# A chain of graph layers on one core: polynomial and convolutions worked pair by pair, with half of each row cast by VectorE and half by ScalarE

## The reference, cut to what matters

```python
# layer 0: attention-like messages, summed by receiver
# layer 1, three passes:
lx = x - spmm(x, src, dst, dinv[src] * w * dinv[dst])
x = hh + proximal_l21(x - lx - hh, gamma * 0.1)
# layer 2, a polynomial of degree 5:
result = c[0] * x; tx = x
for k in range(1, 6):
    tx = segment_sum(norm[:, None] * tx[col], row)   # row = src, col = dst
    result = result + c[k] * tx
# layer 3, twice (relu after the first):
h = x @ W
agg = segment_sum(h[src] * (dinv[src] * dinv[dst])[:, None], dst)
x = agg + h / deg + b
```

## Time and profile before

| | us |
|---|---|
| median of three runs | 8615.32 |
| the profiled execution | 8620.85 |
| its span, first to last instruction | 8619.2 |
| TensorE busy (matmul) | 6966.2 (81%) |
| VectorE busy | 5906.5 (69%) |
| ScalarE busy | 4550.4 (53%) |
| GpSimd busy | 2850.0 (33%) |
| clock granted to TensorE, mean | 0.944 |

### The profile page before, as it was taken

One profiled execution on the slowest core, in us unless ns is written; L12 is line 12 of the kernel. 1 busy time (PEld: TensorE's weight loads), 2 busy tenths in 40 slices (PEclk: granted clock), 3 DMA queues, 4 the chain that ended last, 5 costly groups with the idle time before them and its releaser, 6 DMA issues. The chain is left out here.

```text
span 8619.2 us, 280713 instructions
## 1 busy us (share of the span) xinstructions
PE 6966.2 (81%) x98149; PEld 5903.7 (68%) x98174; DVE 5906.5 (69%) x15840; ACT 4550.4 (53%) x14713; POOL 2850.0 (33%) x2937
## 2 busy tenths in 40 slices
PE   0299999999999899999956886877867787875876
PEld 0155555555555699999956776877867777875866
DVE  1277676766777699898966886886885555555555
ACT  0222222222222499999956997987974444433443
POOL 0078888888888655454530000000000000000000
PEclk9999999999999999999978998999988898987978
DMA  9222222222222377777747887887965454542534
GB/s 385 89 57 61 59 59 60 58 61 58 60 59 59 110 233 232 225 231 223 232 141 232 285 281 244 286 280 253 290 208 167 164 171 157 179 156 90 182 126 134
DMA packets 781195, 1429.84 MB, mean 166 GB/s; under 512 B 294298, under 2 KB 361580, under 8 KB 776696
## 3 DMA queue, kind: packets, MB, share of 16 engines
q1 hardware_dynamic: 571720, 967.63, 36.0%
q10 hardware_dynamic: 116928, 381.29, 12.8%
q0 software_dynamic: 92048, 74.42, 4.4%
HBM read 987.87 MB, written 433.30 MB: 165 GB/s over the span
## 5 line engine op out<-in xcount | busy, mean ns | idle before, releaser
L243 POOL DMA_INDIRECT sorted_rows<-sort_rows,sort_row_at x1600 | 1989.5, 1243 | 518.4 <-issue 507.1
L1458 ACT ACTIVATE smooth_msg<-smooth_ps_l,smooth_w_rows 128x64 f32<-128x64 f32 x7500 | 1592.1, 404 | 229.0 <-PE smooth_ps_l L1522 215.4
L272 ACT ACTIVATE sort_count<-sort_ps_c 50x50 bf16<-50x50 f32 x1600 | 331.2, 207 | 1995.4 <-PE sort_ps_c L304 1559.0
L1216 PE MATMUL poly_ps<-parts,poly_cast 125*128 125x192 bf16 x12500 | 1088.5, 252 | 201.9 <-DVEq L1295 106.3
L1216 PEld LDWEIGHTS poly_ps<-parts,poly_cast 125*128 125x128 bf16 x12500 | 1071.6, 100 | 218.6 <-issue 135.4
L1182 ACT ACTIVATE poly_cast<-poly_mat 128x1280 bf16<-128x1280 uint8 x500 | 609.3, 1262 | 767.9 <-PE poly_ps L1216 520.0
L1522 PE MATMUL smooth_ps_l<-parts,smooth_src 125*128 125x64 bf16 x22500 | 798.5, 194 | 260.5 <-DMA smooth_src<-src_rows 163.7
L1522 PEld LDWEIGHTS smooth_ps_l<-parts,smooth_src 125*128 125x128 bf16 x22500 | 717.7, 99 | 298.0 <-ACT smooth_msg L1458 110.9
L314 PE MATMUL sort_ps_m<-sort_w,sort_hidden 128*125 128x64 f32 x3200 | 879.3, 430 | 0.0
L1536 PE MATMUL smooth_ps_s<-smooth_msg,smooth_hot 128*128 128x64 bf16 x7500 | 760.3, 194 | 143.7 <-DVE smooth_last_part L1670 119.0
L300 PEld LDWEIGHTS sort_ps_r<-sort_count,sort_hot_dt 50*125 50x125 bf16 x1600 | 283.0, 177 | 847.2 <-issue 643.8
...
## 6 DMA issues: line engine op xcount, KB each, us to landing
...
graph_edges<-sorted_rows SPq DMA_DIRECT2D x125, 700.0 KB
...
hot_rows<-graph_hot SPq DMA_DIRECT2D x125, 640.0 KB, 3.4
src_rows<-graph_hot_t SPq DMA_DIRECT2D x125, 640.0 KB, 3.7
```

Of the source, the lines that this page charges most:

```text
L243: pool.indirect_dma_start(out=sorted_rows, out_offset=bass.IndirectOffsetOnAxis(row_at[u][:, j:j + 1], 0), in_=rows[u][:, j, :], in_offset ...
L1216: last = nc.tensor.matmul(ps[u][:, 0:3 * D], cast[u][h][0:NL, s, :], parts[:, b].rearrange("p i d -> p (i d)"), start=b == 0, stop=b == NB ...
L1458: last = act.activation(at[:, s, :], ps_l[g % 2][h][:, i * D:(i + 1) * D], ACT.Copy, scale=w_rows[:, u, c * CHUNK + s:c * CHUNK + s + 1])
```

## The change

What it does:

- **Spilled edges, in all ten passes**: a class `Spilled` works them in rounds of two tiles (250 edges); `n_pairs` is counted beside `n_spilled` in the sort, which also stores one more block of zero rows behind them. GpSimd does the edge load, the cast of the indices, the two gathers, the two additions and the load of `y_sb`; the zeroing of `y_rows` for the next pass follows that load, and the first one stands before the first pass. ScalarE issues the write of the node table.
- **Polynomial and convolutions**: the passes are unrolled, with the structure of smoothing. VectorE casts blocks 0 to 24 of a row in one operation, ScalarE blocks 25 to 49 in one. SyncE issues the loads, each half after its engine's cast of two rows before. The small steps of a finished pair of rows stand behind each cast: four at a time for pairs 6 to 19, all of a pair's for each row of pairs 20 to 24. Spilled edges are worked after pair 2. Rows 0 and 1 of a pass run up to block 47 while the last pairs' steps are still running.
- **A node's own value** is added by TensorE, with an identity, in smoothing and the convolutions.
- **Smoothing**: ScalarE scales the first eight blocks of a chunk, VectorE the last two in one operation, ahead of the second subtraction of the chunk before. The loads are of blocks 0 to 19 and 20 to 49 of a row, with two row buffers; `ADD` is 3; steps stand in pairs 4 to 21 one at a time, in 22 to 24 two at a time.
- `hh` becomes a view of `node_sums`, and `sums` and `rest` share memory with a second `parts`.

The core of the diff:

```diff
@@ sort_edges
-                link(dve.tensor_scalar(pad_f[:], so_far[:], 1.0 / TE, -0.496, ALU.mult, ALU.add), at + 2)
+                dve.tensor_scalar(pad_f[:, 0:1], so_far[:], 1.0 / TE, -0.496, ALU.mult, ALU.add)
+                link(dve.tensor_scalar(pad_f[:, 1:2], so_far[:], 0.5 / TE, -0.498, ALU.mult, ALU.add), at + 2)
...
@@ class Spilled (new)
+    def write_table(self, eng, xs):
+        eng.dma_start(self.rows.rearrange("(p b) d -> p (b d)", b=NB), xs[:].rearrange("p b d -> p (b d)"))\
+           .then_inc(self.table, 16)
+    def on_pool(self, pool, k, n, y_sb):
+        pool.wait_ge(self.table, 16 * k + 16)
+        pool.wait_ge(self.zeroed, 16 * k + 16)
+        with pool.Fori(0, n) as t:
+            m = k * n + t
+            pool.dma_start(self.edges[:], self.sorted_rows[bass.ds(N_SLOTS + t * (2 * TE), 2 * TE), :]
+                           .rearrange("(i p) c -> p i c", i=2)).then_inc(self.got, 16)
+            pool.wait_ge(self.got, m * 16 + 16)
...
+            for i in range(2):
+                pool.indirect_dma_start(out=self.of_node[:, i, :], out_offset=None, in_=self.rows,
+                                        in_offset=bass.IndirectOffsetOnAxis(self.from_at[:, i:i + 1], 0))\
+                    .then_inc(self.fetched, 16)
+            pool.wait_ge(self.ready, m + 1)
+            for i in range(2):
+                pool.indirect_dma_start(out=self.y_rows, ..., compute_op=ALU.add).then_inc(self.added, 16)
+                pool.wait_ge(self.added, m * 32 + (16 * i + 16))
+        pool.dma_start(y_sb[:].rearrange("p b d -> p (b d)"), ...).then_inc(self.y_in, 16)
...
@@ spread
-    N2 = 24
-    DVE_S = 15
+    SPILL_AT, LATE, TWICE = 2, 6, 20
+    EARLY = NB - 2
...
+            def _(sp):
+                def pair(k, p):
+                    for u in two:
+                        for h in two:
+                            if not at_start(k, p):
+                                sp.wait_ge((cast_v, cast_a)[h], number(k, p, u) - 1)
+                                sp.sem_inc(taken, 1)
+                            load(..., u, h)
...
+            def _(act):
+                def pair(k, p):
+                    for u in two:
+                        if not at_start(k, p):
+                            act.wait_ge(row_done, number(k, p, u) - 1)
+                        act.wait_ge(loaded[u][1], k * 16 * PAIRS + 16 * p + 16)
+                        act.activation(cast[u][1][:], mat[u][1][:], ACT.Copy).then_inc(cast_a, 1)
+                for k in range(n_passes):
+                    pair(k, 0)
+                    act.wait_ge(posted, PAIRS * (k + 1))
+                    spilled.write_table(act, xs)
+                    with act.Fori(1, PAIRS) as p:
+                        pair(k, p)
...
+            def _(pe):
+                def first_pair(k):
+                    for u in two:
+                        if k > 0:
+                            pe.wait_ge(row_kept, number(k, 0, u) - 1)
+                        blocks(k, 0, u, 0, EARLY)
+                    pe.wait_ge(posted, PAIRS * k + PAIRS)
+                    for u in two:
+                        last = blocks(k, 0, u, EARLY, NB)
+                        if own_edges:
+                            last = own(k, 0, u)
+                        last.then_inc(row_done, 1)
...
+            def _(dve):
+                def cast_half(k, p, u):
+                    dve.wait_ge(loaded[u][0], k * 16 * PAIRS + 16 * p + 16)
+                    dve.tensor_copy(cast[u][0][:], mat[u][0][:]).then_inc(cast_v, 1)
+                def pair(k, p, by_row, at_once, ahead):
+                    for u in two:
+                        dve.wait_ge(row_done, number(k, p, u) + 1)
+                        dve.tensor_reduce(one_row(sums, p, u), ps[u][0:NL, 0:3 * D]...).then_inc(row_kept, 1)
+                        if not isinstance(p, int) or p < PAIRS - 1:
+                            cast_half(k, p + 1, u)
+                        elif k < n_passes - 1:
+                            cast_half(k + 1, 0, u)
+                        by_row[u].go(at_once)
...
@@ smooth
-    ADD = 2
-    SPILL_AT, LATE, TWICE = 1, 3, 23
+    ADD = 3
+    SPILL_AT, LATE, TWICE = 1, 4, 22
...
-                    for h in two:
-                        act.wait_ge(looked, 2 * number + (h + 1))
-                        for i in range(HALF):
...
+                    act.wait_ge(looked_a, number + 1)
+                    for i in range(BY_ACT):
+                        last = act.activation(at[:, i, :], ps_a[g % 2][:, i * D:(i + 1) * D], ACT.Copy,
+                                              scale=w_rows[u][:, c * CHUNK + i:c * CHUNK + i + 1])
+                    last.then_inc(scaled_a, 1)
...
+                def scale(k, p, u, c):
+                    number = N_CHUNKS * row_of(k, p, u) + c
+                    dve.wait_ge(looked_v, number + 1)
+                    if c == 0:
+                        dve.wait_ge(w_kept, row_of(k, p, u) + 1)
+                    if not (isinstance(number, int) and number < RING):
+                        dve.wait_ge(chunk_done, number - (RING - 1))
+                    dve.tensor_tensor(msg[c][:, BY_ACT:CHUNK, :], ps_v[...]..., w_rows[u][...]..., ALU.mult)\
+                       .then_inc(scaled_v, 1)
...
-                            dve.wait_ge(scaled, 2 * number + 2)
+                            dve.wait_ge(scaled_a, number + 1)
+                            dve.wait_ge(scaled_v, number + 1)
                             dve.tensor_tensor(rest[c][:], msg[c][:], high(msg[c]), ALU.subtract).then_inc(firsts, 1)
+                            if c + 1 < N_CHUNKS or u == 0:
+                                scale(k, p, u + (c + 1) // N_CHUNKS, (c + 1) % N_CHUNKS)
...
@@ polynomial
-            link(dve.tensor_tensor(sums[:], sums[:], y_sb[:], ALU.add))
-            link(dve.tensor_tensor(sums[:], sums[:], wide(dis), ALU.mult))
...
+            link(dve.tensor_tensor(z[:], sums[:, b, :], y_sb[:, b, :], ALU.add))
+            for u in range(2):
+                last = dve.scalar_tensor_tensor(row, z[:, u, :], one_row(by_coeff[:, k, :], p, u), row, ALU.mult, ALU.add)
+            link(last)
+            link(dve.tensor_tensor(xs[:, b, :], z[:], twice[:, b].unsqueeze(2).to_broadcast([NL, 2, D]), ALU.mult))
...
```

776 lines of the change are left out of this document (395 added, 381 removed).

## The result

| | before | after |
|---|---|---|
| median, us | 8612.14 (4 runs) | 8154.54 (4 runs, 8147.68 to 8169.89) |
| ratio | | 0.9472, 95% interval 0.9455 to 0.9488 |
| up to smoothing (profiled execution) | 4500.8 | 4489.3 |
| smoothing, to the next layer norm | 1915.5 | 1768.1 (-147.4; forecast -30) |
| polynomial | 1454.9 | 1228.8 (-226.1; -192) |

Faster by 5.3%. A stage in the table runs from the start of one layer norm to the start of the next. By pass, smoothing took 30.6, 39.4 and 77.4 us less.

What follows compares the result with a forecast made beforehand. It took ScalarE as smoothing's first limit, VectorE close behind, and TensorE, with 70 us a pass not full-rate multiplication, in the polynomial. 8620.85 - 192 (polynomial) - 50 (convolutions) - 30 (smoothing) = 8349, less 5.5: 8343 us; range 8225 to 8450.

Steps and rivals of the forecast that it cites:

- I take 24.1: 12.05 a row: Smoothing's middle rows: VectorE's time for a pair of rows after the change, in us, making VectorE the bound.
- 7 the steps, 0.34 for one between two big ones: Smoothing: of VectorE's 21.8 us a pair before, 7 are small steps, each 0.34 between two big operations.
- 0 to 0.15 per chunk for the second wait: Smoothing: us added to VectorE's time by a second wait ahead of each subtraction.
- 10 x 0.21 to 0.36: Smoothing: us added to VectorE's pair of rows by ten scalings of the last two blocks of a chunk.
- -20 to -25, +18 and +11: Smoothing, us a pass: first eight rows gain 20 to 25, 36 middle rows lose 18, last six lose 11.
- Rival 1: Smoothing: engine waits make the 11.56 us rows, deeper buffers bring 11.2; another -110 us, total 8235; chance 0.14.
- The 4 us for low clock: Polynomial: us charged to each pass for TensorE's lower clock after the short pauses, within the 237.8.
- 38.8 x 5, less 2 at the ends: Polynomial: 38.8 us saved in each of five passes, less 2, giving the stage's -192.
- the 5 for low clock: Convolutions: 5 us added to each for low clock and last steps, within the -25 each.
- rival 2: y_sb lands late, so VectorE waits at pair 6 in polynomial, convolutions and smoothing: +60 us, total 8400; chance 0.18.
- Rival 3: Polynomial and convolutions: VectorE bounds the rows, 4.5 us instead of 4.13; +130 with doubled pairs, total 8475; chance 0.10.
- Rival 4: Smoothing: VectorE, TensorE and ScalarE wait in a ring each chunk, rows of 14.1 us, total 8630; chance 0.04.

Runs made afterwards that it cites:

- run 2: The changed kernel with ScalarE scaling 7 of a chunk's 10 blocks in smoothing and VectorE 3, in place of 8 and 2: 8191.55 us, ratio 0.9512.
- Run 1: The changed kernel with two of smoothing's semaphores counted by 2 and by 3, so waits ask for different values but come no earlier or later: 8256.29 us, ratio 0.9587.
- run 3: The changed kernel with smoothing's row buffers reloaded only after 5 or 7 chunks of the next rows, in place of 2 and 5: 8250.3 us, ratio 0.9573.

## Why the prediction missed, point by point

**The step that failed** is "I take 24.1: 12.05 a row", VectorE's pair of rows in smoothing. It is 21.88. Who bounds the row was right (run 2). Of its terms:
- "7 the steps, 0.34 for one between two big ones": steps priced as the trace of before had them. A step costs 0.09 less ahead of `last_part` in the changed code (0.34, now 0.25) and 0.10 less ahead of `rest` (0.55, from 4906.91 to 4907.46, now 0.45): 14 of them are 1.3 a pair. Between step and big operation the kernel before lists an operation of 46 ns (L1666) or 40 ns (L1669), the changed one none; it has operations of 40 ns at the waits of the scaling instead (L1763, L1767), the first at 4912.6, where `rest` starts. The kernel before:

```profile
4906.91 0.41 DVE L1630 TENSOR_SCALAR xs<-smooth_z,dinv 125x64 f32 x2
L1666 DVEq FUSED_REGOPS  x156: 46/46/81, 4700.0 to 5099.2; - x156
L1669 DVEq ALU_OP  x173: 40/40/40, 4701.1 to 5098.0; - x173
```

- "0 to 0.15 per chunk for the second wait": nothing; behind the step at 4912.18 `rest` starts 0.04 us after its end, and nothing is listed at L1780. Run 1 takes both back at once, and the pair is 23.9, my 24.1; smoothing is then 1865.6 where I forecast 1885.5.
- "10 x 0.21 to 0.36" for the scaling: 0.20, just under the lower bound, which was the reading of the nearest row. I had taken some 0.05 more each: 0.5 a pair.

The step's 1.3, the second wait's 0.7 (run 1's 2.0 less 1.3) and the scaling's 0.5 are 2.5, for the 2.2 that the pair was off; the 0.3 over are not taken apart.

Over the 36 rows of a pass this is 40 us, and passes 0 and 1 came out 30.6 and 39.4 shorter where I had 0. (My own terms for them, -20 to -25, +18 and +11, make +4 to +9 and not 0.) The doubled rows went the same way, 13.2 us for the 14.2 forecast. The two bounds I gave for smoothing (-130 and +90) didn't hold its -147 either: the price of the steps stood in them as fixed. For pass 2, I had 11.0 a row and it was 9.84. Run 1, with the old price of a step, has 10.44 (20.87 / 2), so that price explains 0.6 of the 1.2. The other 0.6 is that I took off only 2.1 a pair for five steps fewer, where run 1 shows 3.0. Rival 1 named the gain and gave the wrong cause, though the deeper buffers are what lets pass 2 have it (run 3).

**Smoothing's first rows**: forecast -20 to -25 us a pass; rows 0 to 7 went from 127.3 to 109.7 in pass 1 and from 127.3 to 111.0 in pass 2, and less in pass 0 (124.4 to 115.3). So the gain was 9 to 18, short of the forecast. The rows themselves are at 10.5 to 17.8, not 10; the transfers of `y_sb`, the zeroing and the table still stand beside them.

**Polynomial, four passes**: 233.5 us each where I had 237.8. By intervals over 4.125, means of the four: boundary 5.1 (4.5), doubled rows 2.9 (4), spilled edges 6.6 (5.5), transfers 5.5 table + 4.2 `y_sb` + 3.0 zeroing = 12.7 (13.5); with 206.3 these make 233.5. The 4 us for low clock have no place beside them. The rows of before show the first half of why. These are PE, PEld, DVE, ACT, POOL, the granted clock, DMA by stretch, around the pause of the earlier trace rows:

```profile
7012.00:7039.00 27.00, 0.90 (x11) 0.67 (x9) 25.18 (x10) 2.43 (x2) 0.00 (x0) 0.55 0.09 30
7039.00:7046.00 7.00, 6.51 (x63) 6.41 (x64) 2.97 (x4) 0.71 (x1) 0.00 (x0) 0.77 0.53 167
7046.00:7053.00 7.00, 7.00 (x88) 7.00 (x86) 2.58 (x4) 2.08 (x3) 0.00 (x0) 1.00 0.67 234
```

Of the 155 us of clock that the stage lost before (0.89 of 1386 us), TensorE was multiplying in 58; in the rest it stood still, as in the four pauses between passes, with 0.54 to 0.62 granted. After a pause of 27 us it lost 0.23 x 7 = 1.6 us. Around the changed boundary:

```profile
6560.00:6565.00 5.00, 2.16 (x18) 2.09 (x19) 4.44 (x17) 0.00 (x0) 0.00 (x0) 0.85 0.50 172
6565.00:6570.00 5.00, 4.62 (x45) 4.30 (x42) 0.69 (x3) 0.13 (x1) 0.00 (x0) 0.81 0.27 102
```

These lose 0.15 x 5 and 0.19 x 5, 1.7 us. The second half of why is in the changed kernel, one pass long:

```profile
6570.00:6800.00 230.00, 213.71 (x2484) 210.62 (x2485) 157.12 (x307) 142.94 (x50) 15.05 (x8) 0.97 0.63 199
```

It does lose 0.03 x 230 = 7 us a pass to the clock, nearly all of it while TensorE multiplies. By the clock's own record these are some 1.7 us each in the intervals at the boundary, at the late table rows, at the spilled edges and at `y_sb` (passes 1 to 3). In the kernel before, the intervals of the earlier trace rows, from which I priced all but the boundary, held such a loss already; I charged it again, beside them.

**The last pass of the polynomial**: "38.8 x 5, less 2 at the ends". With its end it took 217.5 us, 18 less than 237.8 - 2. It has no boundary, no doubled rows at 4.45, no zeroing beside it; its end is 4.0 us. These terms belonged to four passes, not five. **Convolutions**: -82.4 for -50, so 16 more each. Their rows are 4.21, 0.09 over, as forecast (4.1 a pass), and the 5 for low clock is lost (0.98 of 228 us above) but inside the other intervals, as in the polynomial. The transfers were the larger miss: by the intervals, the four first rows of each convolution stood 13.6 to 14.0 us over full rate and now stand 2.3 over, and the two at `y_sb` 8.5 to 9.5 and now 4.2 to 4.6. These are 16 us each where I had 7.

**`y_sb`** (rival 2): no instruction of VectorE waits for `y_sb` in the after trace, and it landed in 12.3 us. GpSimd's part of an addition is longer beside casts, though. One pass, GpSimd in order of time:

```profile
6599.62 2.04 POOL L1189 DMA_INDIRECT y_rows<-poly_total,poly_to  x1 [7.10 <-DVE poly_total L1240]
6604.55 3.29 POOL L1189 DMA_INDIRECT y_rows<-poly_total,poly_to  x1 [2.89 <-DMA y_rows<-poly_total,poly_to]
```

The first addition of each polynomial pass, with no cast beside it, keeps GpSimd busy for 2.04 us, the second, which has one, for 2.86 to 3.56; before it was 2.0 and 3.0. Why it is longer no run here shows, and the 0.8 to 1.5 us a transfer delayed nothing that anything waited for. **Rival 3** (rows of 4.5 in the polynomial) holds in the doubled rows alone. **Rival 4** (ring of waits): rows at 10.9. **The scaling**: an operation lasts 0.28 us and delays the next by 0.20; it is the second that belongs in a sum.
